# Seven block products in place of eight for the attention output product of three head groups

## The reference, cut to what matters

```python
q = (layernorm(x) @ Wq).reshape(b, 112, 4, 8, 128)
k, v = concat(ctx, layernorm(x)) @ Wk, @ Wv        # 487 keys
attn = softmax(q @ k.T / sqrt(128))
out = (attn @ v).reshape(b, 112, 4096)
x = x + out @ Wo                                   # Wo: 4096 x 1024
x = x + ffn(layernorm(x))
```

## Time and profile before

| | us |
|---|---|
| median of 3 runs | 1781.46 |
| the profiled execution, its own time | 1779.8 |
| its span, first to last instruction | 1777.9 |
| around the span (launch and end) | 1.9 |
| TensorE busy | 1761.1 |
| VectorE busy | 864.5 |
| GpSimd busy | 734.5 |
| ScalarE busy | 625.4 |

### The profile page before, as it was taken

One profiled execution on the slowest core, in us unless ns is written; L12 is line 12 of the kernel. 1 busy time (PEld: TensorE's weight loads), 2 busy tenths in 40 slices (PEclk: granted clock), 3 DMA queues, 4 the chain that ended last, 5 costly groups with the idle time before them and its releaser, 6 DMA issues.

```text
span 1777.9 us, 26648 instructions
## 1 busy us (share of the span) xinstructions
PE 1761.1 (99%) x8817; PEld 1552.1 (87%) x8817; DVE 864.5 (49%) x1411; ACT 625.4 (35%) x1238; POOL 734.5 (41%) x588
## 2 busy tenths in 40 slices
PE   9999999999999999999999999999999999999997
PEld 8988988789999989888988898889888989888886
DVE  3611122643343467756775676567655222353247
ACT  3221212233433457504750475047512213212310
POOL 2556461345555545522552355235524222222226
PEclk9999999999999999999999999999999999999999
DMA  9888785257677575512441254125223113111113
GB/s 287 276 282 267 267 290 197 88 184 233 196 251 236 170 236 192 174 60 88 159 136 59 87 162 133 59 87 164 81 71 107 60 44 99 59 48 59 49 57 130
DMA packets 168231, 261.55 MB, mean 147 GB/s; under 512 B 17520, under 2 KB 135536, under 8 KB 167280
## 3 DMA queue, kind: packets, MB, share of 16 engines
q1 hardware_dynamic: 168176, 260.80, 44.5%
HBM read 175.08 MB, written 85.69 MB: 147 GB/s over the span
## 4 chain that ended last, share of the span: by engine, by line
PE 59%; issue 24%; POOL 11%; DMA 2%; DVE 2%; POOLq 1%; ACT 0%; SPq 0%; ACTq 0%; DVEq 0%
PE bank L1398 19%; PE bank L1400 19%; PE bank L1399 19%; POOL tile_region L736 8%; POOL slab_split L670 2%; DMA tile_region<-in_ctxT 1%; DMA k_ctx_scratch<-small_region 1%; DMA slab_raw<-in_wkv 1%; DMA weight_sums_scratch<-slab_raw 1%; PE bank L1717 0%; PE bank L1441 0%; PE bank L1470 0%; POOL slab_raw L700 0%; POOL act_region L689 0%; DVE y_region L1085 0%
## 5 line engine op out<-in xcount | busy, mean ns | idle before, releaser
L736 POOL TENSOR_TENSOR tile_region<-tile_region,small 128x487 f32<-128x487 f32 x224 | 216.7, 1004 | 222.0 <-DVE small L1189 222.0
L1225 DVE TENSOR_TENSOR y_region<-y_region,bank 128x512 f32<-128x512 f32 x308 | 211.2, 687 | 197.4 <-PE bank L1400 197.2
L670 POOL TENSOR_TENSOR slab_split<-slab_raw,slab_split 128x1024 fp32r<-128x1024 f32 x50 | 119.8, 2399 | 308.2 <-ACT slab_split L792 308.1
L1398 PE MATMUL bank<-mid_region 128*128 128x488 f32 (+4 forms) x560 | 227.3, 406 | 1.8 <-DMA mid_region<-k_latents_scratch 1.3
L1400 PE MATMUL bank<-mid_region 128*128 128x488 f32 (+4 forms) x560 | 208.8, 373 | 0.0
L1399 PE MATMUL bank<-mid_region 128*128 128x488 f32 (+4 forms) x560 | 208.8, 373 | 0.0
L1398 PE MATMUL bank<-slab_split,act_region 128*128 128x512 f32 x532 | 207.5, 390 | 0.0
L1400 PE MATMUL bank<-slab_split,act_region 128*128 128x512 f32 x532 | 207.0, 389 | 0.0
L1399 PE MATMUL bank<-slab_split,act_region 128*128 128x512 f32 x532 | 207.0, 389 | 0.0
L1193 DVE TENSOR_REDUCE small<-bank 128x1 f32<-128x487 f32 x224 | 146.0, 653 | 42.8 <-PE bank L1400 42.8
L930 ACT ACTIVATE tile_region<-bank,small 128x487 f32<-128x487 f32 x224 | 153.6, 686 | 27.1 <-DVE small L1193 27.1
(11 more groups left out here) (160 smaller groups left out, 3622.9 us busy)
## 6 DMA issues: line engine op xcount, KB each, us to landing
slab_raw<-in_slabs SPq DMA_DIRECT2D x74, 512.0 KB, 3.5
q_scratch<-y_region SPq DMA_DIRECT2D x16, 1792.0 KB, 7.7
mid_region<-q_scratch SPq DMA_DIRECT2D x32, 896.0 KB, 5.7
slab_raw<-in_slabs SPq DMA_DIRECT2D x80, 256.0 KB, 4.1
weight_sums_scratch<-slab_raw SPq DMA_DIRECT2D x32, 512.0 KB, 4.9
v_scratch<-slab_split SPq DMA_DIRECT2D x8, 1536.0 KB, 8.2
slab_raw<-weight_sums_scratch SPq DMA_DIRECT2D x48, 256.0 KB, 4.2
mid_region<-v_scratch SPq DMA_DIRECT2D x32, 384.0 KB, 3.2
```

The source lines that it names most:

```text
L670: pool.tensor_tensor(WS[s][1], RAWS[raw], f32(WS[s][0]), ALU.subtract).then_inc(s_wlo, 1)
L736: pool.tensor_tensor(PR[i][:, 0:KEYS], PR[i][:, 0:KEYS], rrow[:, i:i + 1].broadcast_to([P, KEYS]), ALU.mult).then_inc(s_pn, 1)
L1225: dve.tensor_tensor(Y[:, r, cols_of(eh)], Y[:, r, cols_of(eh)], gb(c_static)[:, :], ALU.add).then_inc(s_ev, 1)
L1398: pe.matmul(out_ap, w[0], a[0], start=first, stop=False)
```

## The change

Of the seven row tiles of each of the three output products, the first six (768 rows) are taken as a 2 x 2 block matrix: A11, A12 are rows 0 to 383 by the first and second half of the 1024 inner positions, A21, A22 rows 384 to 767; Wo of the group is B11, B12, B21, B22, blocks of 512 x 512. Strassen's scheme in Winograd's form makes the four output blocks from seven block products instead of eight. For that it needs

- four sums of weight blocks, T1 to T4, made by GpSimd in place during the 8 attention steps: each step loads a 512 KB part of the raw weights (two DMAs), makes four 128 x 256 subtractions on it (`output_sums`) and stores the result to DRAM. One of the two buffers is `RAWS[0]`, the other the last eighth of the `Y` region;
- four sums of row blocks, S1 to S4, made by VectorE after the last attention step in 20 instructions of 128 x 768 with both inputs in SBUF (`steps`), each chain in two halves; ScalarE makes their high parts (`sum_hi`), VectorE their low parts (`sum_lo`, 8 more instructions of 128 x 768);
- a changed basis of `Y` for six row tiles, 6 subtractions by GpSimd in group 0 and 6 additions in the last group (`basis`), so that each product is added to at most two places (`take`).

The seventh row tile rides along in four of the seven products as an ordinary product. TensorE's output stage becomes 25 accumulations of 12 matmuls each (`output_products`), in four fixed banks, one for each row tile of the pair. 14 slabs per group are loaded and split in place of 8, with four split buffers (`WW`) in place of two. SyncE's loops over steps are written out. The clearing of the gate region by GpSimd moves from the first attention step of group 0 to the first of group 3.

```diff
+BLOCK_PAIRS = (("A11", "B11", 0), ("A12", "B21", 1), ("A22", "T4", None), ("S3", "T3", None), ("S2", "T2", None),
+               ("S1", "T1", 0), ("S4", "B22", 1))
+PAIR_TILES = [(0, 1, 2) if k is None else (0, 1, 2, 3) for _, _, k in BLOCK_PAIRS]
+PAIR_AT = [sum(len(n) for n in PAIR_TILES[:q]) for q in range(len(BLOCK_PAIRS) + 1)]
+N_WO = PAIR_AT[-1]
+W_SUMS = ("T1", "T4", "T3", "T2")
+N_STEPS = 20
+Y_ORDER = (0, 3, 1, 4, 2, 5, 6)
+ROW_SUMS = ("S3", "S1", "S2", "S4")
...
+def slab_ended(a):
+    return PAIR_AT[a // 2] + 1 if a % 2 == 0 else PAIR_AT[a // 2 + 1]
...
+        WW = WS[0:3] + [[part(RB, S_END, SLAB), part(RA, 2 * NK * ROWS, SLAB)]]
...
+        SUM_RAW = [RAWS[0], part(YR, RT * HID, SLAB)]
+        S_RAW = [part(t, at, ROW_BLOCK // 2).rearrange("p (k n) -> p k n", k=2) for t, at in ((YR, RT * HID), (FB, QT * PP))]
...
+            def load_for_sums(kv, j):
+                buf = SUM_RAW[j % 2].rearrange("p (e k c) -> p e k c", e=2, k=2)
+                for eh in range(2):
+                    slab = slabs[T_WO + NK * kv + 4 * eh + j // 2].rearrange("p (k c) -> p k c", k=2)
+                    sp.dma_start(buf[:, eh, :, :], slab[:, :, 2 * P * (j % 2):2 * P * (j % 2) + 2 * P]).then_inc(s_tld[j % 2], 16)
+            def store_sums(kv, j):
+                sp.wait_ge(s_tsum[j % 2], 4 * (4 * kv + j // 2 + 1))
+                sp.dma_start(t_d[kv, :, j % 2, :, j // 2, :].rearrange("t p c -> p t c"),
+                             SUM_RAW[j % 2].rearrange("p (t c) -> p t c", t=4)).then_inc(s_tst[j % 2], 16)
+            def sums_stored(kv, j):
+                sp.wait_ge(s_tst[j % 2], 16 * (4 * kv + j // 2 + 1))
+            for n in range(1, NKV * B - 1):
+                kv, j = (n - 1) // B, (n - 1) % B
+                sums = kv < NKV - 1
                 sp.wait_ge(s_s, QT * n)
...
+                if j == 0 and kv > 0:
+                    sp.wait_ge(s_mm, C_WO + N_WO * (kv - 1) + PAIR_AT[6])
+                load_qk((n + 1) // B, (n + 1) % B, n + 1, (n + 1) % 2)
+                if sums and j == 0:
+                    sp.wait_ge(s_wlo, P_WO + N_WO_SLABS * kv + 1)
+                    if kv > 0:
+                        sp.wait_ge(s_alo, 8 * kv)
+                    for i in range(2):
+                        load_for_sums(kv, i)
+                if sums and j > 0:
+                    store_sums(kv, j - 1)
                 sp.wait_ge(s_av, 2 * n)
...
+                load_v((n + 1) // B, (n + 1) % B, n + 1, (n + 1) % 2)
+                if kv == 0 and j < RT:
+                    load_y(j)
+                if sums and j > 0:
+                    sums_stored(kv, j - 1)
+                    if j + 1 < B:
+                        load_for_sums(kv, j + 1)
+                if sums and j == B - 1:
+                    next_slab(P_WO + N_WO_SLABS * kv + 2)
+                    store_sums(kv, B - 1)
+                    next_slab(P_WO + N_WO_SLABS * kv + 3)
+                    sums_stored(kv, B - 1)
+                    for a in range(4, N_WO_SLABS + 2):
+                        next_slab(P_WO + N_WO_SLABS * kv + a)
...
-            next_lo(P_WO)
-            p_normalise(1)
-            pool.wait_ge(s_q, N_Q * PAIRS)
+            def wo_lo(kv, a):
+                pool.wait_ge(s_whi, P_WO + N_WO_SLABS * kv + a + 1)
+                w = WW[a % N_WO_SLABS % 4]
+                pool.tensor_tensor(w[1], RAWS[a % 2], f32(w[0]), ALU.subtract).then_inc(s_wlo, 1)
+            def output_sums(kv, j, i):
+                pool.wait_ge(s_tld[j], 32 * (4 * kv + i + 1))
+                W11, W21, W12, W22 = [part(SUM_RAW[j], 256 * k, 256) for k in range(4)]
+                for n, (out, a, b) in enumerate([(W11, W12, W11), (W12, W22, W12), (W22, W22, W11), (W21, W22, W21)]):
+                    if n:
+                        pool.wait_ge(s_tsum[j], 4 * (4 * kv + i) + n)
+                    pool.tensor_tensor(out, a, b, ALU.subtract).then_inc(s_tsum[j], 1)
+            wo_lo(0, 0)
+            def basis(i, eh, op):
+                r = i if eh else 3 + i
+                pool.tensor_tensor(Y[:, r, cols_of(eh)], Y[:, r, cols_of(eh)], Y[:, 3 + i, cols_of(1)], op).then_inc(s_basis, 1)
+            for kv in range(NKV - 1):
+                n = kv * B + 1
+                for j in range(B):
+                    output_sums(kv, j % 2, j // 2)
+                    if j < B - 1:
+                        p_normalise(n + j)
+                    if kv == 0 and j >= 2:
+                        if j % 2 == 0:
+                            pool.wait_ge(s_y[j // 2 - 1], 32)
+                        basis(j // 2 - 1, j % 2, ALU.subtract)
+                wo_lo(kv, 1)
+                wo_lo(kv, 2)
+                p_normalise(n + 7, 0, 4)
+                wo_lo(kv, 3)
+                p_normalise(n + 7, 4)
+                for a in range(4, N_WO_SLABS + 1):
+                    wo_lo(kv, a)
...
+            for i in range(1, B - 1):
                 p_normalise((NKV - 1) * B + i + 1)
+                basis((i - 1) // 2, (i - 1) % 2, ALU.add)
...
+            def wo_hi(kv, a, done):
+                raw, w = a % 2, WW[a % N_WO_SLABS % 4]
+                act.wait_ge(s_raw[raw], 8 * (P_WO + N_WO_SLABS * kv + a) + 16 - 8 * raw)
+                act.wait_ge(s_mm, done)
+                act.activation(w[0], RAWS[raw], ACT.Copy).then_inc(s_whi, 1)
+            def sum_hi(kv, name, h, steps):
+                x = ROW_OPERAND[name]
+                act.wait_ge(s_as, N_STEPS * kv + steps)
+                act.activation(x[0][:, 2 * h:2 * h + 2, :], S_RAW[h], ACT.Copy).then_inc(s_ahi, 1)
+            wo_hi(0, 0, N_UNITS)
             with act.Fori(0, NKV - 1) as kv:
                 with act.Fori(0, B) as b:
                     attention(kv * B + b + 1, b, True, True)
...
+                c0 = C_WO + N_WO * kv
+                def his(first, end):
+                    for a in range(first, end):
+                        wo_hi(kv, a, c0 + (slab_ended(a - 4) if a >= 4 else 0))
+                his(1, 3)
+                sum_hi(kv, "S3", 1, 3)
+                sum_hi(kv, "S3", 0, 6)
+                his(3, 6)
+                sum_hi(kv, "S1", 1, 9)
+                his(6, 7)
+                sum_hi(kv, "S1", 0, 12)
+                his(7, 8)
+                sum_hi(kv, "S2", 1, 14)
+                his(8, 9)
+                sum_hi(kv, "S2", 0, 16)
+                his(9, 12)
+                sum_hi(kv, "S4", 1, 18)
+                sum_hi(kv, "S4", 0, 20)
+                his(12, N_WO_SLABS)
+                wo_hi(kv, N_WO_SLABS, c0 + slab_ended(12))
...
+            def output_products(kv):
+                def steps(h, first, *ops):
+                    for i, (a, b, op) in enumerate(ops):
+                        if first + i:
+                            dve.wait_ge(s_as, N_STEPS * kv + first + i)
+                        a, b = [S_RAW[h] if v is None else f32(v[:, 2 * h:2 * h + 2, :]) for v in (a, b)]
+                        dve.tensor_tensor(S_RAW[h], a, b, op).then_inc(s_as, 1)
+                def sum_lo(name, h):
+                    x = [t[:, 2 * h:2 * h + 2, :] for t in ROW_OPERAND[name]]
+                    dve.wait_ge(s_ahi, 8 * kv + 2 * ROW_SUMS.index(name) + 2 - h)
+                    dve.tensor_tensor(x[1], S_RAW[h], f32(x[0]), ALU.subtract).then_inc(s_alo, 1)
+                def s1(h, first):
+                    steps(h, first, (A21[0], A22[0], ALU.add), (None, A21[1], ALU.add), (None, A22[1], ALU.add))
+                def s2(h, first):
+                    dve.wait_ge(s_alo, 8 * kv + 4 - h)
+                    steps(h, first, (None, A11[0], ALU.subtract), (None, A11[1], ALU.subtract))
+                def s3(h, first):
+                    steps(h, first, (A11[0], A21[0], ALU.subtract), (None, A21[1], ALU.subtract), (None, A11[1], ALU.add))
+                def s4(h, first):
+                    dve.wait_ge(s_alo, 8 * kv + 6 - h)
+                    steps(h, first, (A12[0], None, ALU.subtract), (None, A12[1], ALU.add))
+                def product_done(q, i):
+                    dve.wait_ge(s_mm, C_WO + N_WO * kv + PAIR_AT[q] + i + 1)
+                def add(r, eh, i, op=ALU.add):
+                    return dve.tensor_tensor(Y[:, r, cols_of(eh)], Y[:, r, cols_of(eh)], GB[i][:, :], op)
+                def take(q, i, *adds):
+                    product_done(q, i)
+                    for r, eh, *op in adds:
+                        ins = add(r, eh, i, *op)
+                    ins.then_inc(s_ev, 1)
+                dve.wait_ge(s_avl, 2 + 2 * B * (kv + 1))
+                s3(1, 0)
+                dve.wait_ge(s_tst[1], 16 * 4 * (kv + 1))
+                s3(0, 3)
+                dve.wait_ge(s_basis, 6)
+                dve.wait_ge(s_y[3], 16)
+                take(0, 0, (0, 0), (3, 1))
+                sum_lo("S3", 1)
+                take(0, 1, (1, 0), (4, 1))
+                take(0, 2, (2, 0), (5, 1))
+                sum_lo("S3", 0)
+                take(0, 3, (6, 1), (6, 0))
+                dve.wait_ge(s_alo, 8 * kv + 2)
```

(56 more changed lines are left out.)

121 lines of the change are left out of this document (55 added, 66 removed).

## The result

The changed kernel takes 1823.05 us (median of 4 runs, 1820.62 to 1825.78), the kernel before 1781.18 beside it: ratio 1.0234, 95% interval 1.0216 to 1.0252. It is slower by 42 us. The forecast was 1815 (1792 to 1832), slower with a chance of 0.87; within that range, 1823 lies 1 us above the 1803 to 1822 that had the chance of 0.57. The profiled execution has a span of 1818.7, 40.8 more than before.

What follows compares the result with a forecast made beforehand. TensorE, busy 99% of the span, was taken to bound the kernel. 1779.8 - 24.5 + 49.8 + 6.0 + 2.0 = 1813.1 us profiled; the median stands 1.7 above: 1815 us, range 1792 to 1832.

Steps and rivals of the forecast that it cites:

- -24.5 by 108 matmuls: Output stages: 300 matmuls in place of 336 at 0.227 us each, 8.2 us less a stage, three stages.
- +49.8 by blocking, 16.6 a stage: Output stages: VectorE and GpSimd instructions with two SBUF inputs alternate on one port, so TensorE waits for banks.
- the walk: Instruction-by-instruction timing of an output stage, summing TensorE's waits: 16.6 us with blocking, 2.0 without.
- its check by VectorE's blocked time: Output stage: VectorE blocked 21 us, its chain 49 + 21 = 70 us plus waits, more than TensorE's 68.
- The release 0.13 before the end: Shared SBUF port: a blocked instruction proceeds 0.12 to 0.13 us before the other engine's instruction ends.
- held to the very end: Rival for the output stages: port held for full instruction durations, 19.8 us a stage, 59.4 in all, 1824 us; chance 0.15.
- The store lands near 7, before VectorE wants it at 8: Output stage start: the last weight-sum store, taking 4.9 us from about 1.5, finishes before VectorE needs its buffer.
- little blocking: Rival for the output stages: port sharing costs almost nothing, below 6.2 us lost a stage, time 1769; chance 0.10.
- +6.0 in the first step: Group 0's first attention step: normalisation queued behind output_sums, whose loads come late, delays TensorE by 6.0 us (5 to 8).
- +2.0 by the clock once: After group 0's first-step wait, TensorE's clock falls to 1.2 GHz for 4.1 us, losing 2.0 us (0 to 8).
- a rival at 1825 to 1834: Same blocking, plus up to 6 us for lower clock in stages and 4 for key waits in group 0; chance 0.10.
- 0 for the weight sums in attention: Attention steps beyond group 0's first: GpSimd's subtractions and their loads stay hidden, at most 0.5 us a step, 4 us.

Runs made afterwards that it cites:

- the best version: Changed kernel with attention-output sums in PSUM, step 1's normalisation first, no wait for the last weight-sum store, next group's normalisations behind later splits: 1761.92 us, ratio 0.9892.
- the last run above: The best version without the weight sums' loads, subtractions and stores in attention, plain slabs loaded instead, so output differs: 1760.53 us, ratio 0.9886.

## Why the prediction came right, point by point

- *-24.5 by 108 matmuls.* Right: 8709 matmuls, and the stages of the best version take 69.0 to 70.0 where 68.1 is 300 x 0.227.
- *+49.8 by blocking, 16.6 a stage.* The mechanism is shown: with 24 of 28 instructions off the port the time falls by 36.6 us. The stages of the changed kernel lose 18.1 each (86.2 less 68.1), 1.5 more than forecast. VectorE stood blocked 20.2 us, forecast 21. TensorE's waits by place in the stage of group 1, forecast and measured: pair 1, 6.0 and 4.8; pair 2 and 3, 6.1 and 4.8; pair 5, 4.5 and 1.8. That is 11.4 of the 18.4 of that stage; the other 7 are matmuls at the lower clock and small gaps. As VectorE sets the pace, what it loses shows up as either. Each single wait of the walk was too large, and the lower clock and the gaps that it left out made up for that in the sum, which is luck; what held is its check by VectorE's blocked time.
- *The release 0.13 before the end.* Held: 0.82 from a split's end to the step's, in both cases above, where holding to the very end would make it 0.955. The rival *held to the very end* gave 1824, nearer to the time measured than the forecast's 1815, but by a release that the trace does not show.
- *The store lands near 7, before VectorE wants it at 8.* Wrong in size: VectorE was released by it at 948.88, 8.4 after the start (it took 6.4 from its issue, forecast 4.9), and VectorE idled 1.8 for it. With the port free it costs 4.6 us a stage, and with that wait still there its stages lose 6.4 to 6.8, where the walk without blocking had 2.0 for everything. So the rival *little blocking* had its 1769 too low as well.
- *+6.0 in the first step, +2.0 by the clock once.* 9.7 in the trace, 8.7 by undoing it. The wait was 7.8 against the 1.3 of before, so +6.5. Behind it, from 662.48 to 668.05, the granted clock was 0.50, and 1.00 from there to the stage: 5.6 us at half the speed are 2.8, forecast 2.0. The last 0.3 was there before the wait. Here no other engine sets the pace and the clock costs.
- *The clock in the stages, left out of the sum, and a rival at 1825 to 1834.* The clock did fall there, and the run with matmuls in the waits shows that this cost nothing.
- *0 for the weight sums in attention.* Right within 1.4 to 2.7 us by the last run above.
- *The sum*, 1813.1 for a profiled execution, is 7.5 under the 1820.6 of the one measured (span 1818.7 and 1.9 around it): 4.6 from the stages, 1.7 from the first step, 1.1 from the attention and the rest.

What stays open: why the walk's single waits are up to 2.7 us off while VectorE's blocked time fits; and what keeps VectorE's copies out, when its statistics with one input in SBUF are not. No copy with an end in a bank was tried.
